# Cross-attention and mixture-of-experts kernel: gate weights joined on GpSimd, second selector copies and the third weight piece moved in the prologue

## The chip, the cores and the metric

The program runs on 1 core of one Trainium2 chip. The metric is the device time of one execution in microseconds (us); less is better. The engines are called by the profile's names: PE is TensorE, DVE VectorE, ACT ScalarE, POOL GpSimd, SP SyncE. Every number in the sections ahead of the prediction is from the kernel before the change.

## What is computed

Eight sequences of 512 tokens with 256 features, `x`, and as many context vectors, `ctx`. First a gated cross-attention of mLSTM form with 8 heads, then a gated mixture of 9 experts, two per token:

```python
# gates: one input and one forget gate per head and position
ifg = concatenate([q, k, v], -1)          # q = layernorm(x), k = v = ctx
ig = (ifg @ igate_w.T + igate_b).T;  fg = (ifg @ fgate_w.T + fgate_b).T
cs = cumsum(log_sigmoid(fg), axis=1)
log_D = where(tril, cs[:, :, None] - cs[:, None, :], -inf) + ig[:, None, :]
max_log_D = max(log_D, -1);  D_mat = exp(log_D - max_log_D)
C = qk / sqrt(32) * D_mat
h = (C / (maximum(abs(sum(C)), exp(-max_log_D)) + EPS)) @ v
x = x + tanh(g_xattn) * layernorm(h) * ln_scale
# experts: sigmoid scores, the best two of 9, normalised
x = x + tanh(g_ffn) * sum_e cw[:, e] * (silu(xn @ w1[e].T) * (xn @ w3[e].T)) @ w2[e].T
```

Since k and v are the same array, the rows of the gate weights for k and for v can be added once, ahead of the product.

## The kernel before, in words

The five engines have instruction streams written out by hand, with semaphores between them. SP issues nearly all DMAs in program order; a wait in SP's stream holds up every DMA written behind it. Four stages follow each other:

- **Gates (0 to about 40 us).** The eight sequences are taken in the order 0, 4, 1, 5, 2, 6, 3, 7. SP loads `xa` (x), then small arrays, then `kT` (context, transposed), pair by pair. For step i, DVE takes the mean and variance of `xa` (`a_stats_dve`, L269 and L272), ACT computes the reciprocal deviation (`a_norm_act`, L287, L289), DVE normalises (`a_qn_dve`, L280), PE transposes (`a_pe_turn`, L331) and ACT copies the result to `qT` (`a_qt_act`, L295). After each pair of sequences PE multiplies with the gate weights `wwin` (`a_pe_gates`, L312), all into one PSUM bank. `wwin` is filled with zeros on POOL (L203); then the two halves of the gate weights are copied or added into it (L239, L240), before on DVE between the statistics of the first and of the second sequence. POOL also fills `mx` with zeros (L206, 16 fills) and `asb` with ones (L209).
- **Gate chain (about 40 to 65 us).** ACT and DVE turn the gates into the running sums and maxima (`g_actf_all`, `g_dvef`), POOL splits one row array into three bf16 parts `ap` (`g_pool`), DVE splits another into `mp`. SP writes them to DRAM (`g_sync`, L426 to L433) and reads them back in another layout into `asb` and `mx` (`b_am_sync`, L451, L453), and `EB` (`b_e_sync`, L466). Rows 0 to 11 of `mx` are selector rows that ACT copies (`mx_act`, L246): `mx[0]` serves even batches, `mx[1]` odd ones.
- **Attention (about 65 to 275 us).** 32 tiles t of 128 tokens, four per batch. PE makes the mask exponents (`b_dl_pe`, L528, L530), ACT takes exp (`b_exp_act`, L562), DVE multiplies with the scores (`b_c_dve`, L606), and so on. Beside it runs the weight conversion: the expert weights come as 32 pieces n. SP loads a piece into `wst[n % 2]` (`w_sync`, L477), ACT rounds it to bf16 (`w_hi_act`, L483), POOL computes the rest in three instructions (`w_pool`, L498), and ACT's queue stores both (`w_store`, L489). `w_sync(n)` waits until ACT and POOL have finished piece n-2. Pieces 0 to 3 are loaded and 0 to 2 converted ahead of tile 0; piece 3 is converted in the slot of tile 0, and so on, one a slot.
- **Routing (about 275 to 330 us) and experts (to the end)**, which the change doesn't touch.

The order around the change stands in the programs of the engines at the end of the file: SP writes `w_sync(2)` and `w_sync(3)` ahead of `g_sync`; ACT copies two selector rows after each step of the gate stage; POOL does `w_pool(0)`, `g_pool`, `w_pool(1)`.

## Time and profile before

| | us |
|---|---|
| median of 3 runs | 770.63 (769.81 to 771.09) |
| the profiled execution, its own time | 770.07 |
| its span in the profile | 768.2 |
| PE, DVE, ACT, POOL busy | 650.4, 516.9, 387.7, 410.1 |
| mean granted TensorE clock | 0.826 of full speed |

Times inside the profile run from the first instruction of the span. The profiled execution is 1.9 us longer than its span and 0.56 us under the median of the runs. PE is 85% busy over the whole, but most of that is the expert stage; in the gate chain between 40 and 65 us it stands still but for a few instructions. So the view that matters for this change is the order in time from 0 to 80 us, engine by engine, and the chain that ended last through that stretch.

### The profile page before, as it was taken

What the parts mean: (1) busy time and instruction counts of PE and PEld (TensorE: products, weight loads), DVE (VectorE), ACT (ScalarE), POOL (GpSimd) and SP (SyncE); (2) the same over time, 40 slices, a digit from 0 to 9 for tenths busy, and PEclk for the clock granted to TensorE, in tenths of its full rate; (3) what the DMA queues carried; (4) which work ended last, traced back from release to release, by engine and by line L of the source; (5) the groups of instructions that cost most, each with busy time, mean ns of one, the idle gap of its engine ahead of it and who ended that gap; (6) DMA issues with size and microseconds to landing.
All of it is one profiled execution on the core that took longest, in us unless ns stands there. A gap on an engine that the chain in (4) does not pass through costs nothing.

```text
span 768.2 us, 18534 instructions
## 1 busy us (share of the span) xinstructions
PE 650.4 (85%) x6370; PEld 523.8 (68%) x6370; DVE 516.9 (67%) x1371; ACT 387.7 (50%) x987; POOL 410.1 (53%) x417
## 2 busy tenths in 40 slices
PE   3916799889989850479999999999999999999993
PEld 2412456556656640348989988989899899899892
DVE  8764899898989868934655555555655555655561
ACT  4743778878877740633444443444444334444340
POOL 5062899989999940032353543444544524444423
PEclk9965655575565555599999999999999999999997
DMA  9836798989999721634797896988977968879752
GB/s 299 270 112 165 208 308 276 286 265 288 277 289 316 246 102 14 268 104 148 217 319 231 243 320 208 284 246 253 297 258 214 320 203 277 274 236 302 240 131 45
DMA packets 85820, 179.74 MB, mean 234 GB/s; under 512 B 14881, under 2 KB 48546, under 8 KB 85730
## 3 DMA queue, kind: packets, MB, share of 16 engines
q1 hardware_dynamic: 63202, 140.10, 57.2%
q0 software_dynamic: 13824, 18.43, 11.0%
q10 hardware_dynamic: 8704, 20.06, 6.7%
q8 instruction: 51, 0.84, 0.4%
q14 instruction: 39, 0.32, 0.1%
HBM read 140.93 MB, written 38.67 MB: 234 GB/s over the span
## 4 chain that ended last, share of the span: by engine, by line
PE 56%; POOL 20%; DVE 9%; issue 7%; ACT 3%; DMA 2%; SPq 2%; POOLq 0%; DVEq 0%; ACTq 0%
PE bank L1110 50%; POOL whl L498 8%; POOL x L731 3%; POOL vp L579 2%; POOL qE L595 2%; POOL x L734 2%; PE bank L1104 2%; POOL kw L587 2%; DVE R L1005 1%; PE bank L312 1%; DMA EB<-e_d 1%; ACT qT L295 1%; DVE Qe L1002 1%; PE bank L748 1%; DVE wwin L239 1%
## 5 line engine op out<-in xcount | busy, mean ns | idle before, releaser
L1110 PE MATMUL bank<-xh,w 128*128 128x256 bf16 (+1 forms) x1760 | 268.2, 263 | 9.7 <-DVE xl L1166 6.5
L1092 POOL DMA_INDIRECT out<-res,TS x72 | 115.4, 1602 | 215.2 <-DVE res L1227 142.4
L1110 PE MATMUL bank<-xl,w 128*128 128x256 bf16 (+1 forms) x880 | 222.6, 263 | 0.0
L1183 ACT ACTIVATE sg<-bank 128x256 f32<-128x256 f32 (+1 forms) x240 | 86.8, 362 | 230.2 <-PE bank L1110 226.6
L1110 PEld LDWEIGHTS bank<-xh,w 128*128 128x128 bf16 x1760 | 165.7, 98 | 28.5 <-issue 11.9
L1213 DVE TENSOR_TENSOR hf<-sg,bank 128x256 f32<-128x256 f32 (+1 forms) x200 | 78.9, 394 | 120.9 <-ACT sg L1183 118.1
L1110 PE MATMUL bank<-w,hh 128*128 128x256 bf16 x864 | 140.0, 273 | 0.0
L1083 POOL DMA_INDIRECT xg<-y_d,TG x72 | 72.5, 1006 | 79.0 <-DVE TS L1040 48.4
L498 POOL TENSOR_TENSOR whl<-wst,whl 128x408 bf16<-128x408 f32 x96 | 95.2, 1018 | 35.9 <-ACT whl L483 35.9
L1110 PE MATMUL bank<-w,hlo 128*128 128x256 bf16 x360 | 98.1, 273 | 0.0
L1177 ACT CAST hh<-hf 128x256 bf16<-128x256 f32 (+1 forms) x240 | 90.4, 377 | 12.9 <-DVE hf L1215 11.8
L1110 PEld LDWEIGHTS bank<-xl,w 128*128 128x128 bf16 x880 | 86.3, 98 | 8.2
L1110 PEld LDWEIGHTS bank<-w,hh 128*128 128x128 bf16 x864 | 84.5, 98 | 9.3
L1199 DVE TENSOR_TENSOR hlo<-hf,hh 128x256 bf16<-128x256 f32 (+1 forms) x200 | 78.3, 392 | 0.0
L614 DVE TENSOR_TENSOR Cl<-Cm,Ch 128x512 bf16<-128x512 f32 x64 | 67.3, 1089 | 11.5 <-ACT Ch L568 9.4
L1227 DVE TENSOR_SCALAR res<-bank,cws 128x256 f32<-128x256 f32 x72 | 31.8, 479 | 45.3 <-PE bank L1110 45.3
L528 PE MATMUL bank<-maskb,identb 128*128 128x512 bf16 x64 | 34.8, 544 | 20.6 <-ACT Dm L562 11.3
L568 ACT CAST Ch<-Cm 128x512 bf16<-128x512 f32 x64 | 36.8, 617 | 25.1 <-DVE Cm L606 25.1
L606 DVE SCALAR_TENSOR_TENSOR Cm<-bank,Dm 128x512 f32<-128x512 f32 x64 | 41.1, 683 | 11.8 <-ACT Dm L562 11.7
L748 PEld LDWEIGHTS bank<-wr,yT 128*128 128x128 f32 x128 | 27.2, 297 | 20.8 <-ACT yT L720 11.5
L483 ACT CAST whl<-wst 128x1224 bf16<-128x1224 f32 x32 | 38.7, 1209 | 4.8 <-DMA w_d<-whl 2.6
L562 ACT ACTIVATE Dm<-bank 128x512 f32<-128x512 f32 x64 | 34.0, 578 | 9.7 <-PE bank L530 9.7
(218 smaller groups left out, 1042.5 us busy)
## 6 DMA issues: line engine op xcount, KB each, us to landing
w<-w_d SPq DMA_DIRECT2D x40, 1408.0 KB
w<-w_d SPq DMA_DIRECT2D x40, 768.0 KB
wst<-in_wts SPq DMA_DIRECT2D x32, 612.0 KB, 6.0
w_d<-whl ACTq DMA_DIRECT2D x32, 612.0 KB, 6.9
vb<-in_kv SPq DMA_DIRECT2D x8, 528.0 KB, 5.1
xa<-in_x SPq DMA_DIRECT2D x8, 512.0 KB, 7.9
kT<-in_kv SPq DMA_DIRECT2D x8, 512.0 KB, 8.7
xc<-in_x SPq DMA_DIRECT2D x8, 512.0 KB, 8.1
```

The lines of the kernel that those rows point to most:

```text
L483: nc.scalar.copy(whl[w][:, 0, :], wst[w][:, :]).then_inc(w_hi, 1)
L498: ins = nc.gpsimd.tensor_tensor(whl[w][:, 1, cols], wst[w][:, cols], whl[w][:, 0, cols], ALU.subtract)
L568: nc.scalar.copy(Ch[2 * (t % 2) + g][:, :], Cm[t % 2][g][:, :]).then_inc(b_Ch, 1)
L606: nc.vector.scalar_tensor_tensor(by4(Cm[t % 2][g][:, :]), bank[:, 4:8, g * P:(g + 1) * P], SCALE, by4(Dm[t % 2][g][:, :]), ALU.mult, ALU.m ...
L614: nc.vector.tensor_tensor(Cl[k][:, :], Cm[t % 2][g][:, :], Ch[k][:, :], ALU.subtract).then_inc(b_Cl, 1)
L1083: nc.gpsimd.indirect_dma_start(xg[w][:, j, :], None, y_d, bass.IndirectOffsetOnAxis(ap=TG[:, c0:c0 + 1], axis=0)).then_inc(f_xg[w], 16)
L1092: nc.gpsimd.indirect_dma_start(out, bass.IndirectOffsetOnAxis(ap=TS[:, c0:c0 + 1], axis=0), res[w][:, j, :], None, bounds_check=TOK - 1, o ...
L1110: mm = nc.tensor.matmul(dst, l, r, start=(n == 0), stop=(n == len(pairs) - 1))
L1177: nc.scalar.copy(hh[w][0:K, m, 0:N], hf[m % 3][0:K, 0:N]).then_inc(f_hh, 1)
L1183: nc.scalar.activation(sg[m % 2][0:K, 0:N], bank[0:K, 2 + (NM * w + m) % 4, 0:N], ACT.Silu).then_inc(f_sg, 1)
L1199: V.tensor_tensor(hl_[w][:, m, 0:N], hf[m % 3][:, 0:N], hh[w][:, m, 0:N], ALU.subtract).then_inc(f_hl, 1)
L1213: V.tensor_tensor(hf[m % 3][:, 0:N], sg[m % 2][:, 0:N], bank[:, bk, SLOT:SLOT + N], ALU.mult).then_inc(f_hf, 1)
```

## The change

- **Gate weights.** The four instructions that join the gate weights into `wwin` go from DVE to POOL, between the eight fills of `mx[0]` and the eight of `mx[1]`. They wait for five small loads instead of six.
- **tanh.** The load of `gs` becomes SP's first DMA, with a semaphore of its own; ACT computes `tg = tanh(gs)` first of all, ahead of its wait for the constants.
- **Selector copies.** ACT copies the selector rows of `mx[0]` as before (two after each of the first four steps). The eight copies into `mx[1]` move behind the conversion of piece 2, ahead of the store of piece 1. PE waits for eight copies ahead of tile 0 and for all sixteen ahead of tile 4. The rounding of piece 0 on ACT moves up by one step.
- **Mask rows and pieces.** On SP the load of piece 3 moves from ahead of the DRAM writes of the gate chain to behind the reads of `EB`. On POOL the conversion of piece 1 moves from right behind `g_pool` to behind the first `kw`.

```diff
@@ consts_pool
             for w in range(2):
                 for q in range(2 * HG):
                     nc.gpsimd.memset(mx[w][:, q // HG, q % HG, :], 0.0).then_inc(s_mz, 1)
+                if w == 0:
+                    wwin_pool(pool)
@@
-        def wwin_dve(dve):
-            dve.wait_ge(s_small, 16 * 6)
-            dve.wait_ge(s_wz, 1)
+        def wwin_pool(pool):
+            pool.wait_ge(s_small, 16 * 5)
+            pool.wait_ge(s_wz, 1)
...
-                nc.vector.tensor_copy(dst[:, 0:2, :], gate[:, 0:2, :]).then_inc(s_wwin, 1)
-                nc.vector.tensor_tensor(dst[:, 2:4, :], gate[:, 2:4, :], gate[:, 4:6, :], ALU.add).then_inc(s_wwin, 1)
+                nc.gpsimd.tensor_copy(dst[:, 0:2, :], gate[:, 0:2, :]).then_inc(s_wwin, 1)
+                nc.gpsimd.tensor_tensor(dst[:, 2:4, :], gate[:, 2:4, :], gate[:, 4:6, :], ALU.add).then_inc(s_wwin, 1)
@@ consts_act
-            act.wait_ge(s_small, 16 * 6)
+            act.wait_ge(s_gs, 16)
@@ g_pe_all
-            pe.wait_ge(s_sel, 4 * HG)
+            pe.wait_ge(s_sel, 2 * HG)
@@ b_dl_pe
+            if t == NC:
+                pe.wait_ge(s_sel, 4 * HG)
@@ SP
+            sp.dma_start(gs[:, :], gsc).then_inc(s_gs, 16)
             a_x_sync(sp, ORDER[0])
...
-            sp.dma_start(gs[:, :], gsc).then_inc(s_small, 16)
...
-            for n in range(2, NAHEAD + 1):
-                w_sync(sp, n)
+            w_sync(sp, 2)
             g_sync(sp)
             sp.wait_ge(g_am, 16 * 6)
             sp.wait_ge(s_mz, 4 * HG + 4)
             b_am_sync(sp, 0)
             g_e_sync(sp)
             b_e_sync(sp, 0)
+            for n in range(3, NAHEAD + 1):
+                w_sync(sp, n)
@@ ACT
+            consts_act(act)
             act.wait_ge(s_const, NCONST)
-            consts_act(act)
...
-                mx_act(act, n)
-            w_hi_act(act, 0)
+                if n < HG:
+                    mx_act(act, n)
+                if n == NB - 2:
+                    w_hi_act(act, 0)
             g_actf_all(act)
             b_vh_act(act, 0)
             w_hi_act(act, 2)
+            for n in range(HG, 2 * HG):
+                mx_act(act, n)
             w_store(act, 1)
@@ DVE
             a_stats_dve(dve, 0)
-            wwin_dve(dve)
             a_stats_dve(dve, 1)
@@ POOL
             g_pool(pool)
-            w_pool(pool, 1)
             b_v_pool(pool, 0)
             pool.wait_ge(g_cols, 2)
             b_kw_pool(pool, 0)
-            for n in range(2, NAHEAD):
+            for n in range(1, NAHEAD):
                 w_pool(pool, n)
```

On POOL, in the gate chain, the row of instructions before is this; `whl` is the converted piece, `ap` and `r` belong to `g_pool`, `vp` and `kw` to tile 0.

```order
14 L498 TENSOR_TENSOR whl<-wst,whl 128x408 [waits w_hi,s_lsg]
15 L498 TENSOR_TENSOR whl<-wst,whl 128x408 x2
16 L415 CAST ap<-ga 64x512 [waits g_dve]
17 L417 TENSOR_TENSOR r<-ga,ap 64x512 [waits g_pl]
18 L419 CAST ap<-r 64x512 [waits g_pl]
19 L421 TENSOR_TENSOR ap<-r,ap 64x512 [waits g_pl]
20 L498 TENSOR_TENSOR whl<-wst,whl 128x408 [waits w_hi]
21 L498 TENSOR_TENSOR whl<-wst,whl 128x408 x2
22 L579 TENSOR_TENSOR vp<-vb,vp 128x264 [waits b_vh]
23 L587 TENSOR_TENSOR kw<-vb,col 128x256 [waits b_kv0,g_cols]
```

After the change the same place on POOL reads:

```order
21 L418 CAST ap<-ga 64x512 [waits g_dve]
22 L420 TENSOR_TENSOR r<-ga,ap 64x512 [waits g_pl]
23 L422 CAST ap<-r 64x512 [waits g_pl]
24 L424 TENSOR_TENSOR ap<-r,ap 64x512 [waits g_pl]
25 L584 TENSOR_TENSOR vp<-vb,vp 128x264 [waits b_vh]
26 L592 TENSOR_TENSOR kw<-vb,col 128x256 [waits b_kv0,g_cols]
27 L501 TENSOR_TENSOR whl<-wst,whl 128x408 [waits w_hi]
28 L501 TENSOR_TENSOR whl<-wst,whl 128x408 x2
29 L501 TENSOR_TENSOR whl<-wst,whl 128x408 [waits w_out0,w_hi]
```

Piece 1 has moved from ahead of `vp` to behind `kw`; behind `ap` POOL now waits for ACT's `vp`.

On SP, before, from the loads of `vb` and of pieces 2 and 3 (`wst`) to the writes of the gate chain:

```order
18 L1252 DMA vb<-in_kv 128x4x264
19 L477 DMA wst<-in_wts 128x1224 [waits w_lo,w_hi] x2
20 L426 DMA a_d<-ap 16x4x512 [waits g_pl]
21 L428 DMA m_d<-mp 64x512 [waits g_dve]
22 L431 DMA dec_d<-gdx 64x4 [waits g_act]
23 L433 DMA e_d<-gE 64x512 [waits g_act]
```

After the change, from the last write of the gate chain on SP to the loads for batch 1:

```order
27 L431 DMA m_d<-mp 64x512 [waits g_dve]
28 L454 DMA asb<-a_d 12x2x512 [waits s_mz,g_am]
29 L456 DMA mx<-m_d 3x2x512 x4
30 L442 DMA dec<-dec_d 32x16x4 [waits g_dec]
31 L442 DMA dec<-dec_d 32x16x4 x3
32 L469 DMA EB<-e_d 32x2x512 [waits g_e]
33 L469 DMA EB<-e_d 32x2x512 x3
34 L480 DMA wst<-in_wts 128x1224 [waits w_lo,w_hi]
35 L454 DMA asb<-a_d 12x2x512
36 L456 DMA mx<-m_d 3x2x512 x4
```

The load of piece 3, with its wait for the conversion of piece 1, now stands behind the reads of `EB` instead of ahead of the first write.

On ACT, after the change, from the last instruction of the gate chain to the first exponentials of tile 0 (`Dm`):

```order
43 L366 ACTIVATE col<-bank,neps_c 128x32x8
44 L579 CAST vp<-vb 128x264 [waits b_kv0]
45 L486 CAST whl<-wst 128x1224 [waits w_out0,w_in0]
46 L248 CAST mx<-sel 12x512 [waits s_mz] x8
47 L492 DMA w_d<-whl 256x1x1224 [waits w_hi,w_lo]
48 L567 ACTIVATE Dm<-bank 128x512 [waits b_dl] x2
```

The eight copies into `mx[1]` now stand between the conversion of piece 2 and tile 0; before, the store of piece 1 followed on the conversion directly.

## Rows read from the trace of the kernel before

**Rows 1.** Windows: stretch, busy us and count of PE, PEld, DVE, ACT, POOL; clock, DMA

```profile
64.80:78.60 13.80, 13.80 (x130) 6.56 (x131) 10.19 (x22) 8.59 (x17) 1.99 (x3) 0.50 0.79 202
78.60:270.00 191.40, 168.30 (x1873) 113.12 (x1869) 172.97 (x415) 152.19 (x321) 185.57 (x215) 0.58 0.89 274
```

**Rows 2.** Timeline of POOL and DVE, 0 to 16 us: start, length, instruction

```profile
2.04 7.89 POOL L206 MEMSET mx<- 24x512 bf16 x16
9.89 1.91 POOL L209 MEMSET asb<- 24x512 bf16 x4
...
3.23 0.62 DVE L223 TENSOR_SCALAR maskb<-rowj,pcol 128x128 bf16<-128x128 f32 x1
7.53 4.30 DVE L239 COPY wwin<-wg 128x16 f32<-128x16 f32 x1 [0.95 <-DMA rb<-in_rbias]
12.33 1.35 DVE L280 TENSOR_SCALAR x<-xa,mvA,rsA 128x256 f32<-128x256 f32 x4
13.60 1.40 DVE L269 BATCH_NORM_STATS2 stA<-xa 128x6 f32<-128x256 f32 x4
```

**Rows 3.** Line L258 from 5.5 to 5.8 us: the load of sequence 1, issued 5.58

```profile
DMA to landing us min/median/max: 6.0/6.0/6.0
```

**Rows 4.** Timeline of PE, 16 to 24 us

```profile
16.09 1.97 PE L331 MATMUL bank<-identf,y 128*128 128x128 f32 x8 [1.03 <-DVE y L280]
17.98 2.43 PE L312 MATMUL bank<-kT,wwin 128*32 128x512 f32 x16
...
22.06 1.09 PE L331 MATMUL bank<-identf,x 128*128 128x128 f32 x8
```

**Rows 5.** Timeline of ACT, 37 to 80 us

```profile
37.88 1.13 ACT L246 CAST mx<-sel 12x512 bf16<-12x512 f32 x2
...
55.50 1.22 ACT L483 CAST whl<-wst 128x1224 bf16<-128x1224 f32 x1
65.92 0.60 ACT L562 ACTIVATE Dm<-bank 128x512 f32<-128x512 f32 x1 [9.21 <-PE bank L530]
...
77.38 1.21 ACT L483 CAST whl<-wst 128x1224 bf16<-128x1224 f32 x1
```

**Rows 6.** Timeline of POOL and DVE in the gate chain

```profile
48.85 1.48 POOL L421 TENSOR_TENSOR ap<-r,ap 64x512 bf16<-64x512 f32 x1
50.29 3.22 POOL L498 TENSOR_TENSOR whl<-wst,whl 128x408 bf16<-128x408 f32 x3
...
49.24 3.46 DVE L403 TENSOR_TENSOR g<-cs,gm 64x512 f32<-64x512 f32 x1
52.62 1.43 DVE L405 SCALAR_TENSOR_TENSOR r<-gm,mp 64x512 f32<-64x512 f32 x1
...
54.54 0.68 DVE L409 TENSOR_TENSOR mp<-r,mp 64x512 bf16<-64x512 f32 x1
```

**Rows 7.** Timeline of SP: start and length of the two loads of pieces 2 and 3

```profile
43.15 10.78 SPq L477 DMA_DIRECT2D wst<-in_wts  x2
```

**Rows 8.** Line L428, the three writes of the mask rows: ns to issue, us to land

```profile
L428 SPq DMA_DIRECT2D m_d<-mp x3: 576/593/1316, 54.7 to 59.7; - x3
...
DMA to landing us min/median/max: 2.1/3.1/4.6
```

**Rows 9.** The chain that ended last, in order of time: start, length, what

```profile
59.74 2.05 DMA m_d<-mp
...
66.88 6.46 DMA EB<-e_d
```

**Rows 10.** Timeline of PE and POOL where attention begins

```profile
64.77 0.58 PE L528 MATMUL bank<-maskb,identb 128*128 128x512 bf16 x1 [9.08 <-DMA mx<-m_d]
...
78.67 2.80 POOL L498 TENSOR_TENSOR whl<-wst,whl 128x408 bf16<-128x408 f32 x3 [3.89 <-ACT whl L483]
```

**Rows 11.** Lines L498 and L731, 78 to 270 us: ns min/median/max, first and last start

```profile
L498 POOL TENSOR_TENSOR whl<-wst,whl x85: 947/957/1414, 78.7 to 269.0; 128x408 bf16<-128x408 f32 x85
...
L731 POOL TENSOR_TENSOR x<-x,lsg x29: 719/737/1189, 82.7 to 267.2; 128x256 f32<-128x256 f32 x29
```

More of the change, by code:

```diff
@@ L149, in build @@
         attn_ctx.close()
-        s_iota = sem("s_iota"); s_const = sem("s_const"); s_small = sem("s_small"); s_tanh = sem("s_tanh")
+        s_iota = sem("s_iota"); s_const = sem("s_const"); s_small = sem("s_small"); s_gs = sem("s_gs"); s_tanh = sem("s_tanh")
         s_wz = sem("s_wz"); s_mz = sem("s_mz"); s_sel = sem("s_sel"); s_wwin = sem("s_wwin"); s_lsg = sem("s_lsg")
@@ L249, in lsg_dve @@
             dve.wait_ge(s_tanh, 1)
+            dve.wait_ge(s_small, 16 * 5)
             nc.vector.tensor_scalar(lsg[:, :], lnr[:, :], tg[:, 0:1], None, ALU.mult).then_inc(s_lsg, 1)
         def consts_act(act):
-            act.wait_ge(s_small, 16 * 6)
+            act.wait_ge(s_gs, 16)
             nc.scalar.activation(tg[:, :], gs[:, :], ACT.Tanh).then_inc(s_tanh, 1)
@@ L300, in a_pe_bias @@
         def a_pe_bias(pe):
-            pe.wait_ge(s_small, 16 * 6)
+            pe.wait_ge(s_small, 16 * 5)
             nc.tensor.matmul(GATES, fib_s[0:1, :], ones_row[0:1, :], start=True, stop=False)
```

## Prediction

> **What bounds the kernel now.** I read the windows by stage first. From 78.6 to 270 us POOL is busy 185.57 of 191.40 us: attention runs at POOL's pace, a piece of the weights and the tile's own work in each slot. From 64.8 to 78.6 PE has no gap at all (13.80 of 13.80) at a granted clock of 0.50 [rows 1]. The change adds nothing to POOL's work after 78.6 us, so what it can give is the time by which that stretch starts sooner: what counts is how early PE gets its first mask product (64.77) and POOL the conversion of piece 3 (78.67, released by ACT's rounding of that piece) [rows 10]. After 270 us routing and experts follow, untouched; I let them shift whole.
>
> Then the timelines, engine by engine, up to 80 us. Three places hold up the chain.
>
> The first is at 7.5 us. DVE's copies into `wwin` wait for the sixth small load (7.53), then last 4.30 us, for 16 elements. They end at 11.83, and POOL's fills end at 9.89 + 1.91 = 11.80 [rows 2]: the copies get nothing written until POOL is through. The statistics of sequence 4 are behind them, and the first normalisation starts only at 12.33.
>
> The second is at 49.24 us: DVE's L403, which feeds ACT's `gn`, takes 3.46 us where a subtraction of the same size with POOL idle takes 0.68 (L409). POOL meanwhile does its last `g_pool` step (48.85 to 50.33) and then piece 1 (50.29 to 53.51), and L405 ends at 54.05, 0.54 behind POOL [rows 6].
>
> The third is SP: the entry for the loads of pieces 2 and 3 runs from 43.15 to 53.93, since the second waits for POOL's piece 1 [rows 7]. Only then can the eight writes of the gate chain go out, one after the other; the last mask row is issued at 59.74 and lands 2.05 us later [rows 9]. PE gets `mx` at 64.77, after 9.08 us of idling [rows 10].
>
> **The start.** Taken from DVE: four instructions that stood 4.30 us. Added to POOL: the same four. Their cost on POOL isn't in the trace; four of POOL's shortest comparable instruction, a fill of 7.89 / 16 = 0.49 us, are 2.0 us, and four like L731 (256 columns instead of 16) at 1.189 are 4.8 us; below nothing is excluded, since they are added. I take 2.0, nearer in size. They start at about 8.0, and even with 4.8 us end at 12.8, ahead of the first gate product. POOL's remaining twelve fills (5.9 us) then end at about 16; they are for `mx[1]` and `asb`, which are needed 40 us later.
>
> With DVE free, the first normalisation could start at about 8.7. But step 2's statistics need `xa` of sequence 1, which was issued at 5.58 and landed 6.0 us later, at 11.6 [rows 3]. The new first DMA (`gs`) pushes the stream behind it back by the time of one issue; the same kind of entry costs between nothing (the queue is full anyway) and 0.59 us, the nearest row [rows 8]. I take 0.4: landing at 12.0. Before, these statistics started at 13.60, when DVE got to them, and the first gate product followed at 17.98 [rows 2, 4]. The second normalisation is written behind them on DVE, so its whole chain follows the landing: 13.60 - 12.0 = **1.6 us**. The other 2 us of DVE's gain turn into waiting for the DMA. From 17.98 on PE does pair after pair with hardly a gap, so the shift stays. Bounds: +0.9 more if the second turn's eight transposes run in 1.09 us as the third's do, not in 1.97 [rows 4], and down to a loss of 0.5 (first rival).
>
> Tanh first: ACT loads its table and waits for `gs` alone. It is free by about 6, and its first statistics come at about 7. Nothing, if this cover goes, is late but the normalisation, which has 2 us to spare.
>
> **Selector copies.** Eight copies (four times 1.13 us for two [rows 5]) leave the second half of the gate stage. ACT had to fit them between copies of `qT` for which PE waits only tenths; the rounding of piece 0 fills one of the four gaps again. I take **0.1 us**, between 0 and 0.5. They come back behind piece 2's rounding. L403's end moves from 52.70 to 50.87 (next part), 1.83 earlier, and the rounding from 55.50 to 53.67. It ends at 54.9, and eight copies at 0.52 end at 59.0. Compare that with the first `Dm` below: 59.5. Hidden, by half a microsecond; each microsecond of delay there beyond it counts in full.
>
> **Gate chain and SP.** All on the clock of the trace before; the 1.7 us come off on top. Without piece 1, POOL falls idle at 50.33, and L403 ends 0.54 later, at 50.87. L405 takes 0.68 then: 51.55. L409 ended 55.22 - 54.05 = 1.17 behind L405: the last part of `mp` is there at 52.72, the one before 0.68 sooner, at 52.04. SP is no longer held, so the first five writes are out by then. The second mask row is issued at 52.04, the third `ap` at 52.65, the last mask row at about 53.3 (0.59 each [rows 8]). Before it was 59.74: **6.4 us**. That holds from there to PE's first mask product, 64.77 - 6.4 = 58.4, and to the first `Dm`, 65.92 - 6.4 = 59.5, if the landing again takes 2.1 us; the three of these writes took 2.1, 3.1 and 4.6 [rows 8], and the 4.6 would leave 3.9 of the gain. I take 2.1, the value of the one with a quiet queue behind it, since no piece is loading then. The upper bound is 7.0, with writes that cost SP nothing.
>
> PE then needs the same 13.80 us of work at the same clock, and POOL's piece 3 starts at 78.67 - 6.4 = 72.3.
>
> What is moved in behind: POOL does pieces 1 and 2 from about 55.1, 2.8 us each [rows 10], until 60.7, and `kw` of tile 1 after that; PE wants that `kw` past 68. SP's load of piece 3 is written behind the reads of `EB`, which end at about 60.9; its wait (POOL done with piece 1, 57.9) is over. Queued behind it are batch 1's mask rows and `vb`, none wanted before 80. Piece 3 is wanted by ACT at 77.38 - 6.4 = 71.0: ten microseconds for a load, where the slow `EB` read took 6.46 [rows 9]. The store of piece 1 goes out at 59 instead of 55. Nothing of it is late.
>
> **Sum:** 1.6 + 0.1 + 6.4 = 8.1 us. The profiled execution took 770.07, which gives 762.0; the median of the runs is 0.56 above it: **762.5 us**.
>
> **Rivals.**
>
> *The fills hold the normalisations.* The normalisations (L280) now run beside POOL's later fills. Before, none of the sixteen did (the first at 12.33). For: the copies at 7.53 were held to the end of the fills. Against: L223, of 128 elements, started at 3.23 amid the fills and ended at 3.85, after 0.62 us [rows 2]; large ones get in between two fills. If they are held until the fills end at about 14.6 to 16, PE's first two turns follow back to back, 2 x 1.97, and the gates start at about 18.5 instead of 16.4: 2.1 lost, 764.6. A sentence by itself: the Trainium skill, "SBUF — State Buffer", section "Who interferes with whom", says that `tensor_scalar` can enter a 2-port mode and that it and a GpSimd instruction then shut each other out for a whole instruction; by that rule this rival, or a milder form of it, would come, and the trace agrees with the rule for the copies, more than with "one instruction" even.
>
> *EB or piece 3 late.* In the new order the store of piece 1, the reads of `EB` and the load of piece 3 meet between 59 and 68 us. POOL can stand 3.89 us of lateness in `EB` (its idle time before 78.67 [rows 10]). If the 6.46 us of `EB` double, 2.6 us are lost: 765.1. For: the DMA share in the attention stretch is 0.89 [rows 1]. Against: two loads more in that window is 1.2 MB, at 274 GB/s 4.6 us at the very most, of which 3.9 are covered. The Trainium skill, "DMA: Bandwidth & Descriptors", section "Queues, rings and completion order", has each DMA engine alternate between queues packet by packet, so that ACT's store would slow SP's reads rather than wait behind them; no row here separates the two.
>
> *Quicker turns:* PE's second turn runs at the pace of the third, and the 0.9 of the start comes: 761.6. For: PE now works from the bias product on with fewer gaps ahead of it. Against: a gap of over 2 us stays, while DVE waits for the landing.
>
> *Slower than before: attention falls into a slower rhythm.* POOL's instructions there come in two lengths as they meet DVE: L498 957 or up to 1414 ns, L731 737 or 1189 [rows 11], 0.45 us apart. The medians lie at the short length, so fewer than half are long now. Each slot has one place of either kind, 57 in all; I reckon 33 of them short. The stretch starts from another state of the queues (an extra load, a later store). If all turned long, 14.9 us would be added: 777.4. It decides against the change from 18 of 33 on, since 18 x 0.45 = 8.1. Against: both forms occur in the rhythm of before and are set by POOL's and DVE's own order, which is unchanged after 78 us.
>
> **How the numbers follow.** Forecast 0.62, fills 0.13, late `EB` or piece 0.10, quicker turns 0.10, slower rhythm 0.05 (of which 0.04 beyond the border). The range of 760.6 to 765.5 reaches from 1.9 above the forecast's gain (0.9 + 0.5 + 0.6, the upper bounds) down to both middle rivals, and leaves out the rhythm and the sum of several delays. What a measurement can tell from no change is 0.2%, 1.5 us: faster 0.94, same 0.02, slower 0.04.
>
> **What would show it.** In the profile of the changed kernel: DVE's third group of statistics released by the DMA of `xa` at about 12; the first gate product at 16.4; L403's successor under 2 us long; SP's last write of mask rows at about 51.6 (53.3 less 1.7); PE's first mask product at 56.7; eight selector copies ending within a microsecond of the first `Dm`; POOL's piece 3 at 70.6, still released by ACT, and the same 191 us from there to the end of attention. Wrong would be a normalisation of several microseconds ahead of 16 us, POOL released by `EB` before piece 3, or a longer stretch at POOL's pace.

## The result, and the profile after

| | changed | before, same chip |
|---|---|---|
| median | 764.93 us (763.02 to 767.77, 8 runs) | 770.25 us (767.33 to 773.36, 8 runs) |
| ratio | 0.9931, 95% interval 0.9907 to 0.9955 | |
| profiled execution, its own time | 763.02 us, span 761.2 | 770.07, span 768.2 |

The change gives 5.3 us (3.5 to 7.2 by the interval). Forecast were 762.5 us and a gain of 8.1. The sign and the range (760.6 to 765.5) held; the time came out 2.4 us above the forecast and the gain 2.8 us below it, and one of the three terms had the wrong sign.

Line numbers in the changed kernel are 2 to 5 higher than before (L283 was L280, L334 L331, L406 L403, L501 L498, L533 L528), and those of the experiments differ by a few more. First the timelines of DVE, POOL and PE at the start, in the changed kernel (start, length, instruction, and in brackets the idle time before it and what ended it):

```profile
5.20 1.41 DVE L272 BATCH_NORM_STATS2 stA<-xa 128x6 f32<-128x256 f32 x4 [1.32 <-DMA xa<-in_x]
...
8.64 6.52 DVE L283 TENSOR_SCALAR x<-xa,mvA,rsA 128x256 f32<-128x256 f32 x4
15.08 1.39 DVE L272 BATCH_NORM_STATS2 stA<-xa 128x6 f32<-128x256 f32 x4
```

```profile
2.04 4.17 POOL L206 MEMSET mx<- 24x512 bf16 x8
7.77 0.19 POOL L241 COPY wwin<-wg 128x16 f32<-128x16 f32 x1 [1.56 <-DMA rb<-in_rbias]
7.93 0.21 POOL L242 TENSOR_TENSOR wwin<-wg 128x16 f32<-128x16 f32 x1
8.10 0.19 POOL L241 COPY wwin<-wg 128x16 f32<-128x16 f32 x1
8.25 0.21 POOL L242 TENSOR_TENSOR wwin<-wg 128x16 f32<-128x16 f32 x1
8.41 3.77 POOL L206 MEMSET mx<- 24x512 bf16 x8
12.13 1.91 POOL L211 MEMSET asb<- 24x512 bf16 x4
```

```profile
14.57 1.97 PE L334 MATMUL bank<-identf,x 128*128 128x128 f32 x8 [4.68 <-DVE x L283]
17.56 1.97 PE L334 MATMUL bank<-identf,y 128*128 128x128 f32 x8 [1.02 <-DVE y L283]
19.46 2.99 PE L315 MATMUL bank<-kT,wwin 128*32 128x512 f32 x16
```

Here is the surprise. DVE starts its four normalisations at 8.64, 3.7 us sooner than before [rows 2], but they take 6.52 us instead of 1.35. A window that is open at 8.6 us shows the first of the four alone:

```profile
8.64 5.55 DVE L283 TENSOR_SCALAR x<-xa,mvA,rsA 128x256 f32<-128x256 f32 x1
```

It ends at 14.19, and POOL's last fill ends at 12.13 + 1.91 = 14.04. The other three follow 0.3 us apart. The third statistics (those of sequence 1) then come from DVE's own queue at 15.08 (no DMA in the brackets), and the first gate product is at 19.46: 1.48 us *later* than before [rows 4]. On the other side of the account, the join itself takes POOL 0.69 us, about a third of what was forecast.

The end of the gate chain, on DVE, SP, PE and ACT:

```profile
50.91 1.63 DVE L406 TENSOR_TENSOR g<-cs,gm 64x512 f32<-64x512 f32 x1
52.47 0.67 DVE L408 SCALAR_TENSOR_TENSOR r<-gm,mp 64x512 f32<-64x512 f32 x1
...
53.63 0.69 DVE L412 TENSOR_TENSOR mp<-r,mp 64x512 bf16<-64x512 f32 x1
```

```profile
41.85 0.34 SPq L480 DMA_DIRECT2D wst<-in_wts  x1
...
53.63 0.45 SPq L431 DMA_DIRECT2D m_d<-mp  x1
54.12 1.29 SPq L429 DMA_DIRECT2D a_d<-ap  x1
55.45 0.68 SPq L431 DMA_DIRECT2D m_d<-mp  x1
```

```profile
56.46 3.20 ACT L248 CAST mx<-sel 12x512 bf16<-12x512 f32 x6
...
59.57 1.13 ACT L248 CAST mx<-sel 12x512 bf16<-12x512 f32 x2
61.92 0.60 ACT L567 ACTIVATE Dm<-bank 128x512 f32<-128x512 f32 x1 [1.22 <-PE bank L535]
```

```profile
60.77 0.58 PE L533 MATMUL bank<-maskb,identb 128*128 128x512 bf16 x1 [5.23 <-ACT mx L248]
```

```profile
74.66 2.79 POOL L501 TENSOR_TENSOR whl<-wst,whl 128x408 bf16<-128x408 f32 x3 [3.93 <-ACT whl L486]
```

L406 takes 1.63 us for 3.46 [rows 6], SP no longer stands for 10.78 us [rows 7], the last mask row goes out at 55.45 for 59.74 [rows 9], and PE's first mask product and POOL's piece 3 come 4.0 us sooner each [rows 10]. From there to the end of attention the windows by stage:

```profile
61.90:74.66 12.76, 12.76 (x130) 6.40 (x130) 10.19 (x22) 8.65 (x17) 3.23 (x5) 0.50 0.92 252
74.66:266.10 191.44, 172.02 (x1876) 115.53 (x1872) 174.30 (x419) 152.37 (x322) 187.14 (x217) 0.56 0.89 278
```

PE is again without a gap in the first, and POOL sets the pace in the second (187.14 us busy of 191.44). The bounds of these windows were chosen, so their widths are no measurement. How long the stretch is shows on POOL, from the conversion of piece 3 to that of the last piece, 31, before and changed:

```profile
269.02 3.24 POOL L498 TENSOR_TENSOR whl<-wst,whl 128x408 bf16<-128x408 f32 x3
```

```profile
263.77 3.23 POOL L501 TENSOR_TENSOR whl<-wst,whl 128x408 bf16<-128x408 f32 x3
```

That is 190.35 us before and 189.11 in the changed kernel. The rest of the 7.0 us between the two profiled spans comes later: the first expert matmul is at 329.9 us in this kernel and at 335.2 before, 5.3 sooner, and the expert stage from there on takes 431.3 us for 433.0. So of the 7.0 us 4.0 are there at piece 3, 1.2 come in the attention and 1.7 in the expert stage; more on the last two below.

### The profile page after: what moved, and what is told of

Its sections match the earlier page's. It is cut to its first block, busy times and chain, and to the rows that moved or that the text cites. A ratio compares the mean times of both kernels' runs of the same rounds, so it can differ in the third digit from the quotient of the medians.

```text
span 761.2 us, 18534 instructions
## 1 busy us (share of the span) xinstructions
PE 652.5 (86%) x6370; PEld 524.8 (69%) x6370; DVE 516.0 (68%) x1367; ACT 388.0 (51%) x987; POOL 410.1 (54%) x421
## 4 chain that ended last, share of the span: by engine, by line
PE 50%; POOL 20%; DVE 10%; issue 9%; DMA 6%; ACT 2%; SPq 1%; POOLq 0%; DVEq 0%; ACTq 0%
PE bank L1115 44%; POOL whl L501 8%; DMA out<-res,TS 5%; POOL x L736 3%; POOL vp L584 2%; POOL qE L600 2%; POOL x L739 2%; PE bank L315 2%; POOL kw L592 2%; PE bank L1109 1%; DVE R L1010 1%; DVE x L283 1%; DVE xl L1171 1%; DVE Qe L1007 1%; PE bank L334 1%
## 5 line engine op out<-in xcount | busy, mean ns | idle before, releaser
L501 POOL TENSOR_TENSOR whl<-wst,whl 128x408 bf16<-128x408 f32 x96 | 94.9, 1014 | 30.9 <-ACT whl L486 30.8
L533 PE MATMUL bank<-maskb,identb 128*128 128x512 bf16 x64 | 35.7, 558 | 12.2 <-ACT Dm L567 6.9
L511 PE MATMUL bank<-qT,kT 32*128 32x128 f32 x512 | 39.2, 450 | 0.0
```

The lines of the kernel that those rows point to most:

```text
L501: ins = nc.gpsimd.tensor_tensor(whl[w][:, 1, cols], wst[w][:, cols], whl[w][:, 0, cols], ALU.subtract)
L511: mm = nc.tensor.matmul(bank[:, 4 + j, g * P:(g + 1) * P], kT[rows, b, c, g * P:(g + 1) * P], qT[rows, b, c, g * P:(g + 1) * P], start=Tru ...
```

## The experiments

Theory, called A in some of the expectations: POOL's twelve later fills hold the normalisation until the last of them is through. A1 is its narrower form: only fills that follow without a gap shut DVE out. The rivals put the lateness on something else at that time: the join, tanh and table loads on ACT, the DMA stream. All kernels are the changed one with the edit shown. The marks in time are from one profiled execution each. "Piece 3" is POOL's first conversion in attention, [rows 10] for the kernel before.

| kernel | third statistics | first gate product | first mask product | piece 3 | profiled execution |
|---|---|---|---|---|---|
| before | 13.60 | 17.98 | 64.77 | 78.67 | 770.07 |
| changed | 15.08 | 19.46 | 60.77 | 74.66 | 763.02 |
| fills behind the gate stage | 11.86 | 16.25 | 57.55 | 71.44 | 764.02 |
| fills spaced | 12.02 | 17.04 | 57.58 | 71.47 | 761.04 |
| normalisation with two inputs | 12.05 | 16.59 | 58.04 | 71.93 | 763.48 |
| eight fills halved | 13.39 | 17.78 | 58.48 | 72.38 | 761.40 |
| four fills more | 16.90 | 21.29 | 61.74 | 75.63 | 767.17 |
| join back on DVE | 13.60 | 17.99 | 58.13 | 72.03 | 761.03 |
| all copies stepped | 15.14 | 19.53 | 60.86 | 74.75 | 765.75 |
| piece 1 early | 15.22 | 19.61 | 64.84 | 78.73 | 767.97 |
| piece 1 and load 3 early | 14.93 | 19.32 | 66.70 | 80.59 | 776.89 |
| fills behind, `gs` behind | 11.74 | 16.13 | 56.28 | 70.18 | 759.69 |

**1. Fills behind the gate stage.**

```diff
             wwin_pool(pool)
+            pool.wait_ge(a_q, NB * NC)
             for q in range(2 * HG):   # mx[1]
```

> The changed kernel, with POOL's twelve later fills (mx[1], asb) moved behind the last normalisation. Theory A (DVE's normalisation is held by POOL's back-to-back fills until the last one ends, 8.64 to 14.19 us): no normalisation lasts longer than 0.45 us, the third group of statistics starts when xa of sequence 1 lands, near 12.0, the first gate product at about 16.4 instead of 19.46, and piece 3 on POOL at about 71.5 instead of 74.66; time 3.1 us under the changed kernel. Theory B (the delay is the landing of the data or DVE's own order): first gate product stays within 0.5 us of 19.46 and the time is that of the changed kernel.

Measured: 761.89 us (759.27 to 764.02), before 770.14; ratio 0.9893 (0.987 to 0.9915). DVE:

```profile
8.53 1.35 DVE L284 TENSOR_SCALAR x<-xa,mvA,rsA 128x256 f32<-128x256 f32 x4
11.86 1.40 DVE L273 BATCH_NORM_STATS2 stA<-xa 128x6 f32<-128x256 f32 x4 [1.98 <-DMA xa<-in_x]
```

This is the start as it was forecast: four normalisations in 1.35 us, the third statistics released by the landing of `xa` at 11.86 (forecast 12.0), the gate product at 16.25 (forecast 16.4). It is 3.2 us sooner than in the changed kernel, and piece 3 is 3.2 us sooner too. Between the two marks it isn't level: ACT takes up the gates 2.4 us sooner (39.47 for 41.84), mostly since the first group of gate products takes 3.64 us here and 2.99 there, and the gate chain gives the rest back (18.08 us for 18.93 from there to the first mask product). The median is 3.0 us under that of the changed kernel, expected were 3.1; the two come from different sets of runs, and the intervals of their ratios just overlap.

**2. Fills spaced:** each later fill waits until the one before it is written.

```diff
                 for q in range(2 * HG):
+                    if w:
+                        pool.wait_ge(s_mz, 2 * HG + q)
                     nc.gpsimd.memset(mx[w][:, q // HG, q % HG, :], 0.0).then_inc(s_mz, 1)
```

(and likewise for the four of `asb`)

> The changed kernel, with each of POOL's twelve later fills waiting for the one before it to be complete, so that none stands ready behind another. Theory A1 (what shuts DVE out is the unbroken sequence: the next fill is there before the one before has ended): DVE gets in at a gap, the first normalisation ends within 1 us of 8.64 and all four by about 11; first gate product near 16.4. Theory A2 (POOL keeps DVE out as long as it has any fill to do): first normalisation ends only behind the last fill, at 14.2 or later, first gate product at 19.5 or later.

Measured: 761.04 us, one run. DVE and POOL:

```profile
8.71 2.23 DVE L286 TENSOR_SCALAR x<-xa,mvA,rsA 128x256 f32<-128x256 f32 x4
```

```profile
8.44 4.66 POOL L208 MEMSET mx<- 24x512 bf16 x8
13.16 2.30 POOL L214 MEMSET asb<- 24x512 bf16 x4
```

The same twelve fills at the same place, 0.58 us apart instead of 0.47, and the four normalisations take 2.23 us instead of 6.52. So a fill that is running doesn't hold DVE for long; what does is that the next one stands ready: A1. The gaps cost something all the same: the second normalisations take 2.18 us (1.35 in experiment 1), and the gate product is at 17.04, expected was 16.4.

**3. Normalisation with two inputs:** same arithmetic, the reciprocal deviation given as a second, broadcast tensor.

```diff
-                nc.vector.tensor_scalar(qn[...], xa[n][:, c, :], mvA[:, t, 0:1], rsA[:, t:t + 1],
-                                        ALU.subtract, ALU.mult).then_inc(a_q, 1)
+                nc.vector.scalar_tensor_tensor(qn[...], xa[n][:, c, :], mvA[:, t, 0:1],
+                                               rsA[:, t:t + 1].to_broadcast([P, D]), ALU.subtract, ALU.mult).then_inc(a_q, 1)
```

> The changed kernel, with the normalisation written as a scalar_tensor_tensor (reciprocal deviation as a second, broadcast tensor input) instead of a tensor_scalar; fills as changed. Theory A (a one-input form takes both of DVE's port pairs and is shut out by fills, a two-input form only shares reads, and fills read nothing): no hold; the four take about 1.4 us from 8.64, first gate product near 16.4. Theory C (any DVE write of this size is shut out by the fills): the first ends at 14.2 as in the changed kernel, first gate product at 19.5.

Measured: 763.48 us, one run. DVE:

```profile
8.71 1.64 DVE L283 SCALAR_TENSOR_TENSOR x<-xa,mvA,rsA 128x256 f32<-128x256 f32 x4
12.05 1.41 DVE L272 BATCH_NORM_STATS2 stA<-xa 128x6 f32<-128x256 f32 x4 [1.71 <-DMA xa<-in_x]
```

The fills run unbroken beside it (8.54 to 14.18) and hold nothing; against 1.35 us in experiment 1, four take 0.3 us more in this form. The form of the DVE instruction decides. The Trainium skill, "SBUF — State Buffer", section "Who interferes with whom", has it so: single-input `copy`, `cast` and `tensor_scalar` can take the port pair that DVE shares with GpSimd, and a two-input instruction contends only with a GpSimd instruction that reads SBUF, which a fill doesn't. By that rule this form would be free, and the trace agrees: 1.64 us for four. Where the page has the blocked engine wait for the whole of one instruction, the changed kernel shows twelve (5.55 us).

**4 and 5. The dose.** The eight fills of `mx[1]` as half as many elements of twice the size; and four fills more among them, into a buffer that nothing reads.

```diff
-                    nc.gpsimd.memset(mx[w][:, q // HG, q % HG, :], 0.0).then_inc(s_mz, 1)
+                    dst = mx[w][:, q // HG, q % HG, :]
+                    nc.gpsimd.memset(dst.bitcast(F32) if w else dst, 0.0).then_inc(s_mz, 1)
```

> The eight fills of mx[1] are written as 256 fp32 elements instead of 512 bf16, so that each stores the same bytes with half as many elements; all else as changed. If a normalisation waits until GpSimd's unbroken row of fills ends, a shorter row (eight fills in about 1.9 us for 3.77) frees it about 1.9 us sooner: first normalisation ends at 12.3 (14.19 in the changed kernel), third group of stats at 13.3 (15.08), first gate product about 17.7 (19.46), piece 3 at about 72.9 (74.66). If a normalisation instead gets past a fixed number of fills, or waits for the bytes written and not for time, nothing moves: 19.5 and 74.7. Time about 761.5 to 764 by the first, 763 to 765 by the second.

```diff
                     nc.gpsimd.memset(mx[w][:, q // HG, q % HG, :], 0.0).then_inc(s_mz, 1)
+                    if w and q < 4:
+                        nc.gpsimd.memset(more[:, q, :], 0.0).then_inc(s_more, 1)
```

> Four further fills of the same shape (24x512 bf16, into a buffer that nothing reads) stand between the first fills of mx[1], 1.9 us of GpSimd; all else as changed. If a normalisation waits for the end of the row of fills, everything behind it is 1.9 us later: first normalisation ends at 16.1, third group of stats at 17.0, first gate product 21.3, piece 3 at about 76.5, profiled time about 765. If it is held by something that ends at 14 whatever GpSimd does (a transfer, ScalarE's reciprocal roots), the four fills change nothing: 19.5 and 74.7.

Measured: 761.40 and 767.17 us, one run each. The first normalisation of the halved one, and of the one with more, by windows open at 8.6 us:

```profile
8.65 3.86 DVE L284 TENSOR_SCALAR x<-xa,mvA,rsA 128x256 f32<-128x256 f32 x1
```

```profile
8.60 7.42 DVE L286 TENSOR_SCALAR x<-xa,mvA,rsA 128x256 f32<-128x256 f32 x1
```

They end at 12.51 and 16.02; the last fills end at 12.36 and 15.87. With the 14.19 against 14.04 of the changed kernel, that is three times 0.15 us behind the last fill. The gate product came at 17.78 and 21.29, expected were 17.7 and 21.3. At piece 3 both are sooner than expected, by 0.5 and 0.9 us (72.38 for 72.9, 75.63 for 76.5): behind ACT's take-up of the gates the changed kernel's trace is 0.7 to 0.8 us slower than theirs (18.93 us to the first mask product, 18.10 and 18.19 in these). The times of the profiled executions miss their expectations, 761.5 to 764 and about 765, by 0.1 and 2.2 us; that is the spread of the stages behind, told below.

**6. Join back on DVE**, all else as changed: the four instructions of `wwin_pool` on VectorE between the first two groups of statistics.

> The changed kernel, with the four instructions that join the gate weights back on DVE between the statistics of sequence 0 and 4 (they wait for five small loads); everything else as changed. Theory A: DVE's copies are held from about 7.8 to the end of the sixteen plus four fills at 11.8, the first normalisation starts at 12.3, the first gate product at 18.0 and piece 3 at 73.2: 1.5 us faster than the changed kernel. So the move of the join by itself is a loss of 1.5 us. Theory B (the move of the join was neutral or a gain, and the first load of gs delayed the start): first gate product at 19.5 or later, time not below the changed kernel.

Measured: 762.66 us (761.03 to 766.29), before 770.14; ratio 0.9922 (0.99 to 0.9945). The copies are held as before (`7.73 4.11`), the gate product is at 17.99, as before the change, and piece 3 at 72.03 (expected 73.2), 2.6 us sooner than in the changed kernel. Of these 1.5 are there at the first gate product, 0.4 come from a shorter first group of products (2.56 for 2.99) and 0.7 from a shorter gate chain (18.19 for 18.93), which the join has no part in. By the profiles the join on POOL is a loss, as long as the fills stand behind it. The run also shows the gate chain by itself: from the same gate product as before, the mask product and piece 3 come 6.64 us sooner each (58.13 for 64.77, 72.03 for 78.67). The two medians (762.66 and 764.93) come from different sets of runs, and their intervals overlap; the size rests on the profiles.

**7. Piece 1 early:** its conversion on POOL back right behind `g_pool`.

```diff
             g_pool(pool)
+            w_pool(pool, 1)
             b_v_pool(pool, 0)
```

> The changed kernel, with POOL's conversion of piece 1 back right behind g_pool; SP's load of piece 3 stays behind the reads of EB. Theory A (the gain behind the gates has two parts: DVE meets no piece, and SP isn't held): DVE's L406 lasts 3.4 us instead of 1.63 and the third part of mp is done 2.5 us later, SP's last mask row goes out about 2.1 us later (57.5 instead of 55.45) and PE's first mask product about 62.9 instead of 60.77. Theory B (only SP's wait mattered): both stay within 0.5 us of the changed kernel.

Measured: 767.97 us, one run. DVE:

```profile
51.93 3.46 DVE L406 TENSOR_TENSOR g<-cs,gm 64x512 f32<-64x512 f32 x1
55.32 1.43 DVE L408 SCALAR_TENSOR_TENSOR r<-gm,mp 64x512 f32<-64x512 f32 x1
```

The 3.46 and 1.43 us of before return to the hundredth [rows 6], beside `52.98 3.22` of piece 1 on POOL. L406 starts 1.02 later than in the changed kernel, the first mask product 4.07 later (64.84, expected 62.9); the difference, 3.0 us, is what piece 1 costs by this pair. A closer pair is this kernel and that of experiment 9: ACT takes up the gates at 42.86 in both, and the first mask product is at 64.84 and 60.86, 4.0 us apart. Of these, 2.6 are there when SP issues the last mask row (58.37 and 55.78), as much as L406 and L408 take longer, and 1.4 come behind it: the row takes 3.5 us to land for 2.1. Why it lands later wasn't tested.

**8. Piece 1 and load 3 early:** `w_sync(3)` back ahead of `g_sync` on SP as well.

> The changed kernel, with both the conversion of piece 1 and the load of piece 3 back where they were. Theory A: the gate chain loses all of its 5.8 us on the clock from the end of the gates: PE's first mask product at about 66.6 instead of 60.77, piece 3 on POOL at 80.5 instead of 74.66; time 770.8, that of the kernel before or slightly slower (the start is 1.8 us later than before). Theory B (the gain came from the copies or the tanh): first mask product below 64.

Measured: 772.07 us (770.47 to 776.89, 13 runs), before 769.17; ratio 1.0031 (1.0016 to 1.0046): slower than before. SP:

```profile
42.12 13.73 SPq L480 DMA_DIRECT2D wst<-in_wts  x2
55.91 0.64 SPq L429 DMA_DIRECT2D a_d<-ap  x1
...
61.15 0.59 SPq L431 DMA_DIRECT2D m_d<-mp  x1
```

SP's old wait is back, and it costs more than the lateness of DVE that it runs beside: the first mask product is 5.9 us later than in the changed kernel, 5.7 after allowing for the 0.26 that L406 is later. So by the changed kernel's trace the move of the pieces is worth 5.7 us: 3.0 from POOL and 2.6 more from SP. By the eight other traces with the pieces moved, whose gate chains are 0.7 to 1.0 us shorter, it is 6.4 to 6.6: 3.8 to 4.0 and 2.6. Without it the change is a loss, since the start costs 1.5 us.

**9. All copies stepped:** all sixteen selector copies in the gate stage again.

> The changed kernel, with all sixteen selector copies back in the gate stage, two a step (the rounding of piece 0 stays where the change has it). Theory A (ACT's eight copies end 1.2 us ahead of the first Dm, and PE waits little for ACT in the gate stage): gates done at most 0.5 us later, ACT idle more ahead of the first Dm, piece 3 between 74.6 and 75.2. Theory B (the copies stand in the way in one of the two places): piece 3 over 1 us off 74.66.

Measured: 765.75 us, one run. At the mask product and at piece 3 it is level with the changed kernel (0.09 us), as expected of copies that are worth nothing. The stretches between say otherwise: ACT takes up the gates 1.0 us later, where at most 0.5 was expected. From the first product of the second pair to ACT's take-up of the gates (the first row of each fence below to the second) it takes 17.17 us here:

```profile
25.69 1.92 PE L315 MATMUL bank<-kT,wwin 128*32 128x512 f32 x16
...
42.86 0.59 ACT L344 ACTIVATE g<-bank 64x512 f32<-64x512 f32 x1 [1.01 <-PE bank L315]
```

and 15.84 in the changed kernel:

```profile
26.00 1.92 PE L315 MATMUL bank<-kT,wwin 128*32 128x512 f32 x16
...
41.84 0.59 ACT L344 ACTIVATE g<-bank 64x512 f32<-64x512 f32 x1 [2.04 <-PE bank L315]
```

The other traces of this study with the new place of the copies show 15.84 or 15.85, but for experiment 3 with its slower normalisations (16.43); before it was 16.07. So all sixteen copies in the gate stage, with the rounding of piece 0 one step earlier, cost 1.3 us there; PE now waits 1.08 us for ACT's `qT` ahead of the last group of products (40.87). Moving the copies off gave 0.2 against before. By piece 3 alone the 1.3 don't show, because of two things that go against the changed kernel's trace: 0.4 us more from its first to its second pair and 0.9 more in its gate chain. The run answers one question more. In the changed kernel PE's first mask product is put down to ACT's copies, which end at 60.70. Here those copies are long done, and it is at 60.86 all the same:

```profile
60.86 0.58 PE L533 MATMUL bank<-maskb,identb 128*128 128x512 bf16 x1 [4.29 <-DMA mx<-m_d]
```

The program says the same: ahead of tile 0 PE waits for eight copies, and these were made in the gate stage; the eight that end at 60.70 are waited for only ahead of tile 4. So the release was the read of `mx`; the copies only ended beside it.

**10. Fills behind, `gs` behind:** the first experiment, and SP's load of `gs` behind the small ones.

```diff
-            sp.dma_start(gs[:, :], gsc).then_inc(s_gs, 16)
             a_x_sync(sp, ORDER[0])
...
             sp.dma_start(rb[:, :], rbias).then_inc(s_small, 16)
+            sp.dma_start(gs[:, :], gsc).then_inc(s_gs, 16)
```

> The kernel with the fills behind the normalisations (first gate product 16.25, piece 3 at 71.44), with the load of gs back behind the other small ones, on its own semaphore. Theory A (the landing of xa of sequence 1 sets the start, and the first DMA pushed it back by the time of an issue): first statistics 0.4 us sooner, third group near 11.5, first gate product 15.9, piece 3 at 71.1. ACT's tanh comes at about 7.5 and its two table loads end at 10.4, past the first statistics. Theory B (then ACT is the bound): first normalisation at 10.9, but the third group still at 11.5 to 12.3; first gate product 16.2 or later.

Measured: 760.41 us (759.65 to 763.96), before 769.17; ratio 0.989 (0.9866 to 0.9915). DVE and POOL:

```profile
9.62 1.38 DVE L284 TENSOR_SCALAR x<-xa,mvA,rsA 128x256 f32<-128x256 f32 x4 [1.35 <-ACT rsA L293]
11.74 1.40 DVE L273 BATCH_NORM_STATS2 stA<-xa 128x6 f32<-128x256 f32 x4 [0.74 <-DMA xa<-in_x]
```

```profile
70.18 2.80 POOL L502 TENSOR_TENSOR whl<-wst,whl 128x408 bf16<-128x408 f32 x3 [3.45 <-ACT whl L487]
```

The landing of `xa` is only 0.12 us sooner, although ACT is now later with the first reciprocal deviations (1.35 us of waiting, all of it covered). So `gs` in front costs 0.1 us at the gates, where 0.4 was expected. The median is the lowest of all, 8.8 us under before, where the change gives 5.3; but its ratio isn't apart from that of experiment 1 (0.9893). Piece 3 comes 1.3 us sooner than in experiment 1, more than the 0.12 explain: the first group of gate products takes 2.80 us here and 3.64 there, and ACT takes up the gates at 38.32 instead of 39.47. What sets the length of that group wasn't tested. From the first gate product to the second pair it takes 6.0 to 7.4 us in the twelve traces, so that single traces can't settle a difference of less than a microsecond behind the gates.

## Why the prediction was right, and where it was wrong

**Start: forecast +1.6, measured -1.5.** This is the step that failed: the sum let the first normalisation run at about 8.7 unhindered, on the argument that "large ones get in between two fills". What happened is the first rival, "The fills hold the normalisations", which had a chance of 0.13. The argument rested on L223 [rows 2], an instruction of DVE that got in after 0.62 us amid the fills. That row was read rightly. In the changed kernel, too, DVE's first constants come through while POOL fills, and the first two fills of `mx[0]` beside them take 661 and 662 ns, the last four 514:

```profile
1.36 0.73 POOL L203 MEMSET wwin<- 128x768 f32 x1
```

```profile
1.51 0.67 DVE L221 CAST rowjb<-rowj 128x128 bf16<-128x128 f32 x1
1.59 0.66 DVE L222 TENSOR_SCALAR identf<-rowj,pcol 128x128 f32<-128x128 f32 x1
2.17 0.62 DVE L223 TENSOR_SCALAR identb<-rowj,pcol 128x128 bf16<-128x128 f32 x1
...
2.77 0.62 DVE L225 TENSOR_SCALAR maskb<-rowj,pcol 128x128 bf16<-128x128 f32 x1
```

POOL's row of fills starts at 1.36, with that of `wwin`, and those of `mx[0]` follow without a gap. DVE's cast arrives at 1.51 amid the first of them and is through at 2.18, 0.09 us behind its end (before the change it took 1.13 us, one fill more); from there the two engines get through side by side. The copies at 7.53 [rows 2] also arrived amid a row, and were held 4.3 us until the last fill, as the normalisations then were. So the same trace held one row for the term and one against it, both arrivals in an unbroken row of fills, and I took the one without being able to say what parts them. That is still open: the fill running at 1.51 was one of 128 partitions, the later ones of 24, and which of this or something else decides wasn't tested. Experiments 2, 4 and 5 show that a gap between the fills ends the hold and that the last fill sets its length, for DVE instructions that arrive later than 7 us.

The rival's mechanism was right, its price of 2.1 us under the forecast start too small: measured are 19.46 - 16.25 = 3.2. I had PE's two turns follow back to back. But the third statistics are written behind the held normalisations on DVE, so the second turn comes 3.0 us after the first, not 2.0. The other terms of the start hold: landing 11.86 for 12.0, gate product 16.25 for 16.4 once the fills are away. The join's cost of 2.0 us was 0.69. In the sum it lay beside other work, but once the fills hold DVE it counts: they stand behind the join and ended at 14.04, where the prediction had "about 16". The rival's 18.5 was reckoned from the early end of its 14.6 to 16. Tanh first cost 0.1 of the 0.4 allowed.

**Selector copies: forecast 0.1, measured 0.2** (16.07 to 15.84, experiment 9). The eight moved ones end 1.22 us ahead of the first `Dm`; forecast was half a microsecond, at 0.52 us a copy, where the rows cited have 1.13 for two; measured are 4.24 for eight.

**Gate chain and SP: forecast 6.4, measured 5.8.** L406 starts 1.67 us later than L403 did before; the lateness of 1.48 at the first gate product has become 1.81 when ACT takes up the gates (41.84 for 40.03), since the first group of products is 0.56 us longer and the copies give 0.2. With that taken off, L406 ends at 50.73, forecast 50.87. It ends 0.54 us behind POOL's last `g_pool` step, the same distance as before, on which that step of the forecast rested. The 0.6 us that are missing are two small things: a write of `ap` rows that held SP for 1.29 us, so that the last mask row goes out at 53.6 on the clock of before instead of 53.3, and 5.32 instead of 5.03 us from there to the first mask product. They seem to belong to this trace more than to the change: from ACT's take-up of the gates to the mask product it takes 24.74 us before (40.03 to 64.77), 18.93 here (41.84 to 60.77), and 17.96 to 18.19 in experiments 1 to 6, 9 and 10, a term of 6.6 to 6.8, close above the forecast. Experiments 7 and 8 split it, within a microsecond, into 3.0 to 4.0 from POOL and 2.6 from SP. In the changed kernel's trace 5.8 - 1.8 = 4.0 are left at the mask product and at piece 3.

**Attention shifts whole: right within 1.2 us.** ACT releases piece 3, `EB` isn't late (1.89 us of waiting for it at 69.02, none of it in front of piece 3), and no slower rhythm came: from piece 3 to piece 31 it takes 189.1 to 190.4 us in the twelve traces, 190.35 before and 189.11 in the changed kernel. Behind piece 3 POOL waits for ACT's rounding for 3.5 us before and 2.0 in the changed kernel. Before and changed stand at the two ends of that spread, but experiment 2, with the change in it, takes 190.35 like before; I can't put the 1.2 us down to the change.

**The end: not forecast, and not the change's.** The span is 7.0 us shorter, though only 5.3 of it are there at the first expert matmul. Two windows of 5 us at the same work, before and changed:

```profile
345.00:350.00 5.00, 4.32 (x25) 3.21 (x26) 0.93 (x3) 0.38 (x1) 1.89 (x2) 0.67 0.79 314
```

```profile
339.70:344.70 5.00, 4.36 (x40) 3.94 (x41) 1.64 (x5) 1.29 (x4) 1.89 (x2) 1.00 0.79 311
```

PE is as busy in both, but with 25 matmuls in the one and 40 in the other: the granted clock (the column before the DMA share) is 0.67 there, so part of the stretch ran at the lower of its two levels, 1.2 GHz, shortly after PE had waited for DVE at the start of that stage (4.1 us in two waits, in the changed kernel as well). Such a dip comes in some executions and not in others, though the code of that stage is the same in all kernels: the expert stage takes 431.2 or 431.3 us in six of the twelve traces, the changed kernel's among them, 432.9 to 434.4 in five, and 438.2 in that of experiment 8. That is why single times differ by more than the forecast's terms, and why the marks in time are the sharper measure. The 764.02 us in experiment 1 are an execution with such a dip (434.4 us from the first expert matmul on); its piece 3 is 3.2 us ahead of the changed kernel's.

In sum at piece 3, in us sooner than before: -1.48 (start), -0.56 (the first group of products), +0.23 (copies), +5.81 (chain), 4.00 in all, for 8.1 forecast. The median's 5.3 lies between that and the 7.0 of the profiled pair; with the gate chain of the eight other traces the 4.0 would be 4.7 to 5.0, an estimate. With the fills out of the way (experiment 1) the gain at piece 3 is 7.2, and 8.5 in experiment 10. The rival's 764.6 came close to the measured 764.93, partly by luck: of the 6.0 us that it left for piece 3 only 4.0 were there in the profiled pair, and its own price was too small by a microsecond. The range held because it was drawn to take this rival in; the measured time lies 0.6 us inside its upper end. (Its lower end, 760.6, is 1.9 under the forecast, while the three gains named for it add up to 2.0.)

## What to carry to other kernels

When an instruction moves to another time, look at what the engine it shares a port with does at its *new* time. If the trace has rows for and against a hold and you can't say what parts them, the unfavourable one deserves more than a small chance, and the experiment that parts them (a gap, or the work moved away) should come first. A row of cheap fills on GpSimd that nobody needs soon belongs behind the latency chain, or needs a gap between its members; here moving it gave 3.2 us at the first gate product, twice what the join on POOL had lost with the fills behind it. In a handwritten queue, writes that another engine waits for go ahead of loads that wait themselves: the move of the pieces on SP and POOL gave 5.7 us or more, and of this change's other parts only the copies gave anything, 0.2.

## What the runs showed of the hardware

- Single-input VectorE instructions (`tensor_scalar` on 128x256 fp32, also a copy of 16 elements) that arrived later than 7 us in an unbroken row of GpSimd fills on 24 partitions were held to the end of the row: the first `tensor_scalar` took 3.86, 5.55 and 7.42 us by the row's length and ended 0.15 us behind it. With each fill waiting for its predecessor, four took 2.23 us. The form with two inputs wasn't held (1.64 for four). Nor was the row of constants that arrived at 1.51 amid a fill on 128 partitions: its cast was through after 0.67 us. What parts the cases is open.
- Beside GpSimd `tensor_tensor` instructions, which read SBUF, a two-input VectorE instruction (L406) took 3.46 us in all three traces where such instructions went on until it had ended, and 1.63 where the last of them ended 0.54 us before it.
- Four GpSimd instructions on 16 columns took 0.69 us; a fill of 512 bf16 elements came every 0.47, one of 256 fp32 every 0.26.
- The first sixteen gate products took 2.43 to 3.64 us in these traces, the groups of the later pairs 1.92, with the granted clock column at 1.00 for all; what slows them wasn't tested.
